# Scan stage: ScalarE's first tap issued in front of the older head's square, and the last output projection split, with its weights in another buffer

## The reference, cut to what matters

```python
H, P, N, G, K, CH, E = (32, 128, 128, 8, 4, 32, 256)   # 32 heads of width 128, 8 groups
proj = x @ in_proj_w.T                    # gate, (hidden, B, C), dt
hbc = silu(causal_conv(hbc, conv_w, K taps) + conv_b)
hs, B, C = split(hbc)
dt = softplus(dt + dt_bias)
# per head: a scan in chunks (inside a chunk by matmuls, from chunk to chunk by states)
y = (Y_diag + Y_off) + D * hs
h32 = y * silu(gate)                                  # per head, 1024 tokens x 128
g = h32.reshape(b, s, 8, 512)                         # 4 heads make one norm group
var = mean(g * g, axis=-1)
h32 = g * rsqrt(var + EPS)
return norm_w * h32 @ out_proj_w.T                    # 4096 -> 256, added to x
```

## Time and profile before

| | us |
|---|---|
| median of 3 runs | 1653.99 (1649.94 to 1654.58) |
| the profiled execution, its own time | 1655.48 |
| its span, first to last instruction | 1653.7 |
| share of the span in which PE, DVE, ACT, POOL were busy | 87%, 69%, 53%, 30% |
| the scan's heads in steady work (1010 to 1514 us): PE, DVE, ACT, POOL busy | 473.2, 387.6, 330.2, 290.3 of 504 |
| the end of the scan (1526 to 1549 us): PE, DVE busy | 17.4, 7.5 of 23 |

### The profile page before, as it was taken

One profiled execution on the slowest core, in us unless ns is written; L12 is line 12 of the kernel. 1 busy time (PEld: TensorE's weight loads), 2 busy tenths in 40 slices (PEclk: granted clock), 3 DMA queues, 4 the chain that ended last, 5 costly groups with the idle time before them and its releaser, 6 DMA issues. The chain is left out here.

```text
span 1653.7 us, 25033 instructions
## 1 busy us (share of the span) xinstructions
PE 1437.4 (87%) x7896; PEld 1056.5 (64%) x7896; DVE 1139.2 (69%) x2026; ACT 878.2 (53%) x1238; POOL 497.1 (30%) x407
## 2 busy tenths in 40 slices
PE   3999489999999966994997968899999999998697
PEld 3788343333333345883786757788887887887586
DVE  5622599989989847332775756777776777867475
ACT  2422227767767744322434765667575665755332
POOL 1444210000000113542001114655645556564100
PEclk9999759999999977997997998999999999999899
DMA  8532211111111028334001103222322222221200
GB/s 296 146 52 46 58 31 21 23 25 20 27 28 27 5 96 286 52 52 120 2 0 40 42 25 91 83 90 90 96 77 85 77 96 90 84 90 39 77 1 26
DMA packets 83030, 112.06 MB, mean 68 GB/s; under 512 B 11905, under 2 KB 60801, under 8 KB 82913
## 3 DMA queue, kind: packets, MB, share of 16 engines
q1 hardware_dynamic: 73152, 96.05, 19.5%
q0 software_dynamic: 9376, 14.16, 4.8%
q10 hardware_dynamic: 384, 0.39, 0.1%
HBM read 89.99 MB, written 11.93 MB: 62 GB/s over the span
## 5 line engine op out<-in xcount | busy, mean ns | idle before, releaser
L962 DVE TENSOR_REDUCE attn_max_chunks<-attn_scores 128x1 f32<-128x512 f32 x488 | 305.4, 684 | 30.7 <-PE attn_scores L1213 25.2
L1124 ACT ACTIVATE attn_probs<-attn_scoresT 128x1024 f32<-128x1024 f32 x256 | 248.2, 1022 | 118.8 <-PE attn_scoresT L1229 118.6
L1213 PE MATMUL attn_scores<-attn_k_picks,attn_q_group 64*128 64x512 f32 x488 | 188.5, 466 | 14.5 <-DVE attn_max_chunks L962 6.0
L1213 PEld LDWEIGHTS attn_scores<-attn_k_picks,attn_q_group 64*128 64x128 f32 x488 | 85.7, 191 | 178.5 <-DVE attn_max_chunks L962 170.4
L1644 DVE SCALAR_TENSOR_TENSOR ssm_scan_x<-ssm_scan_proj,ssm_w_conv,ssm_scan_x 128x1023 f32<-128x1023 f32 (+2 forms) x96 | 123.1, 1282 | 84.1 <-ACT ssm_scan_x L1639 78.4
L1229 PE MATMUL attn_scoresT<-attn_q_group,attn_k_picks 64*128 64x512 f32 x512 | 153.9, 438 | 3.3 <-ACT attn_probs L1124 3.3
L1241 PE MATMUL attn_o<-attn_probs,attn_v_group 128*32 128x512 f32 x1024 | 139.2, 616 | 0.4 <-ACT attn_probs L1124 0.3
L62 PE MATMUL ssm_scan_proj<-ssm_xnT_hi,ssm_w_in_hi 128*128 128x512 f32 x256 | 111.0, 434 | 27.8 <-DVE ssm_scan_x L1644 22.5
L293 POOL DMA_INDIRECT moe_sums<-moe_xn,moe_token x46 | 77.7, 1690 | 128.4 <-DVE moe_xn L430 122.6
L2481 PE MATMUL ssm_scan_out<-ssm_scan_w_out,ssm_scan_v 128*128 128x256 f32 x480 | 110.7, 384 | 4.6 <-POOL ssm_scan_w_out L2186 4.4
L481 ACT ACTIVATE moe_xnT<-moe_gate 128x512 f32<-128x512 f32 x46 | 27.5, 597 | 153.6 <-PE moe_gate L64 153.6
(11 more groups left out here) (355 smaller groups left out, 3400.5 us busy)
## 6 DMA issues: line engine op xcount, KB each, us to landing
ssm_cum_all<-ssm_cums SPq DMA_DIRECT2D x32, 512.0 KB, 3.7
ssm_scan_exp_cum<-ssm_cums SPq DMA_DIRECT2D x32, 512.0 KB, 3.7
moe_w_gate_lo<-in_moe_w SPq DMA_DIRECT2D x16, 512.0 KB, 11.2
moe_w_up_lo<-in_moe_w SPq DMA_DIRECT2D x16, 512.0 KB, 11.1
moe_w_down<-in_moe_w SPq DMA_DIRECT2D x16, 512.0 KB, 11.1
ssm_w_in<-in_in_w SPq DMA_DIRECT2D x64, 128.0 KB, 2.6
ssm_scan_w_out<-in_out_w SPq DMA_DIRECT2D x8, 512.0 KB, 3.8
moe_sums<-main_residual SPq DMA_DIRECT2D x2, 1024.0 KB, 5.6
```

Source lines behind the costliest of these rows:

```text
L962: return nc.vector.tensor_reduce(rmaxc[:, half, place:place + 1], chunk_bank(g, n), AX_X, ALU.max).then_inc(reduced, 1)
L1124: nc.scalar.activation(probs[s % 2][:, 2 * pair:2 * pair + 2, :], st_ps[pair][:], ACT.Exp, scale=SCALE).then_inc(exp_done, 1)
L1213: nc.tensor.matmul(chunk_bank(g, n), qs[b][head_rows(j), t * P:(t + 1) * P], kz[b][head_rows(j), j % 2, c * BANK:(c + 1) * BANK], start=Tr ...
```

## The change

First, in ACT's list `square` of head n-1 moves from behind `ahead(n)` to behind the first tap inside `ahead(n+1)`, so that tap comes in front of square. Second, the last group's output weights go to the buffer of `grow` (`w_out_last`), loaded once the last `cgrow` is done, and `scale_out(7)` scales them there. Third, PE's last projection first does heads 28 to 30 for pairs 0 and 1, then head 31 for them, then `norm_sums` into `y_ps`, then pairs 2 and 3.

```diff
+        w_out_last = grow[:].rearrange("p (j d) -> p j d", j=NORM_HEADS)
...
             def load_out(gw):
-                if after(gw, 1):
+                if is_at(gw, G - 1):
+                    sync.wait_ge(q["cgrow_done"], HM)
+                elif after(gw, 1):
                     sync.wait_ge(q["out_mm"], PAIRS * gw)
...
-                sync.dma_start(w_out[:], src).then_inc(w_out_in, 16)
+                sync.dma_start(w_out_last if is_at(gw, G - 1) else w_out[:], src).then_inc(w_out_in, 16)
...
-                nc.vector.tensor_copy(sums[:], out_ps[1][:, 0, 0:TT]).then_inc(q["sums_done"], 1)
+                nc.vector.tensor_copy(sums[:], y_ps[:, 0:TT] if is_at(gw, G - 1) else out_ps[1][:, 0, 0:TT]).then_inc(q["sums_done"], 1)
...
-            def ahead(n, j, gw, norm_of=None):
+            def ahead(n, j, gw, norm_of=None, square_of=None):
                 tap(n, j)
+                if square_of is not None:
+                    square(*square_of)
                 grow_of(n)
...
             def body(n, j, gw):
+                passed = (n - 1, (j - 1) % G, gw - (j % NORM_HEADS == 0)) if after(n, 1) else None
                 if not is_at(n, LAST):
-                    ahead(n + 1, j + 1, gw + (j % NORM_HEADS == NORM_HEADS - 1), gw - 1 if j % NORM_HEADS == 0 and after(n, 1) else None)
-                square(n, j, gw)
+                    ahead(n + 1, j + 1, gw + (j % NORM_HEADS == NORM_HEADS - 1),
+                          gw - 1 if j % NORM_HEADS == 0 and after(n, 1) else None, passed)
+                else:
+                    square(*passed)
...
             heads(act, body)
+            square(LAST, LAST % G, G - 1)
             norm(G - 1)
...
+            def project_last(p, heads_of):
+
+                first, end = heads_of[0] == 0, heads_of[-1] == NORM_HEADS - 1
+                for m in range(2):
+                    cols = slice((2 * p + m) * P, (2 * p + m + 1) * P)
+                    for jn in heads_of:
+                        last = nc.tensor.matmul(tail_ps[p][:, m, :], v[:, v_row((G - 1) % 2 * NORM_HEADS + jn), cols], w_out_last[:, jn, :],
+                                                start=(first and m == 0 and jn == 0), stop=(end and jn == NORM_HEADS - 1),
+                                                skip_group_check=True)
+                if end:
+                    last.then_inc(q["out_mm"], 1)
...
-            for p in range(PAIRS):
-                for m in range(2):
-                    project_out(G - 1, (G - 1) % 2, p, m, tail_ps[p])
-                if p == 0:
-                    norm_sums(G - 1)
+            pe.wait_ge(q["w_out_scaled"], G)
+            pe.wait_ge(q["v_done"], LAST)
+            pe.wait_ge(q["added"], PAIRS * (G - 1))
+            for p in range(2):
+                project_last(p, range(NORM_HEADS - 1))
+            pe.wait_ge(q["v_done"], HM)
+            for p in range(2):
+                project_last(p, (NORM_HEADS - 1,))
+            norm_sums(G - 1)
+            for p in range(2, PAIRS):
+                project_last(p, range(NORM_HEADS))
```

More of the change, by code:

```diff
@@ L2185, in scale_out @@
                 pool.wait_ge(w_out_in, 16 * (gw + 1))
-                nc.gpsimd.tensor_tensor(w_out[:], w_out[:], norm_w[:, bass.ds(gw * NORM_HEADS, NORM_HEADS)]
+                w = w_out_last if is_at(gw, G - 1) else w_out[:]
+                nc.gpsimd.tensor_tensor(w, w, norm_w[:, bass.ds(gw * NORM_HEADS, NORM_HEADS)]
                                         .unsqueeze(2).broadcast_to([P, NORM_HEADS, D]), ALU.mult).then_inc(q["w_out_scaled"], 1)
@@ L2460, in norm_sums, with project_out @@
                 pe.wait_ge(q["summed"], SUMS * (gw + 1))
-                if after(gw, 1):
+                if is_at(gw, G - 1):
+                    pe.wait_ge(q["y_done"], HM)
+                elif after(gw, 1):
                     pe.wait_ge(q["added"], PAIRS * gw)
+                dst = y_ps[:, 0:TT] if is_at(gw, G - 1) else out_ps[1][:, 0, 0:TT]
                 for t in range(TT):
-                    last = nc.tensor.matmul(out_ps[1][:, 0, t:t + 1], squares[:, t * P:(t + 1) * P], ones[:, 0:1],
+                    last = nc.tensor.matmul(dst[:, t:t + 1], squares[:, t * P:(t + 1) * P], ones[:, 0:1],
                                             start=True, stop=True)
                 last.then_inc(q["norm_mm"], 1)
-            def project_out(gw, b, p, m, out=None):
+            def project_last(p, heads_of):
[8 more added lines that the diff above has]
+                    last.then_inc(q["out_mm"], 1)
+            def project_out(gw, b, p, m):
                 if p == 0 and m == 0:
@@ L2471, in project_out @@
                     pe.wait_ge(q["v_done"], NORM_HEADS * (gw + 1))
-                if m == 0 and out is None and (p >= 2 or after(gw, 1)):
+                if m == 0 and (p >= 2 or after(gw, 1)):
                     pe.wait_ge(q["added"], PAIRS * gw + p - 1)
-                if m == 0 and out is not None and p == 0:
-                    pe.wait_ge(q["added"], PAIRS * gw)
                 if p == 1 and m == 0:
                     pe.wait_ge(q["sums_done"], gw + 1)
-                out = out_ps[p % 2] if out is None else out
+                out = out_ps[p % 2]
                 cols = slice((2 * p + m) * P, (2 * p + m + 1) * P)
```

## The result

Two comparisons on the chip, each with the kernel before beside it. In the first the changed kernel took 1630.32 us (median of 4, 1624.36 to 1631.37), before 1654.28, a ratio of 0.9835 [0.9803, 0.9867]. In the second it took 1627.88 us (median of 5, 1623.88 to 1631.66), a ratio of 0.9836 [0.9813, 0.9860]. By the ratios the change takes 27 us off (23 to 31 in the second comparison), by the medians 24.0 and, against 1654.34 for before, 26.5; 20.2 were forecast. The direction was right and the size too small. The profiled executions stand at 1653.7 and 1628.3 us of span, 25.4 apart.

A forecast was written before the change was run, and what follows sets the result against it. The prediction saw a circle through ACT, DVE and PE, with PE's floor at 15.14 us a head. Scan 13.7 plus end 6.5 made 20.2 us off: 1634 us, 8 in 10 within 1628 to 1643.

The forecast's parts named there:

- step 1: Heads 1 to 3: earlier taps cut PE's gaps from 3.40 to 2.43 us, gate projections stay slow; 2.9 us gained.
- the end: End of the scan: early last weights and new product order bring DVE's last additions 6.5 us earlier; bounds 4.5 and 6.8.
- heads 27 and 28: Written-out end of a group: the load starts from PE's quarter's end, so an earlier tap gains 0 us.
- Step 2: Loop middle heads: 16.07 us becomes 15.20, a gain of 0.87 in each of 8, 7.0 us.
- the circle: Chain through the heads: v, square and tap, DVE's taps, gate projection, chunk states, next v; forecast 0.97 us shorter.
- Step 3: Written-out middle heads: 15.33 to 15.20 us, 0.13 in each of 5, 0.65 us.
- Step 5: Last heads of groups: 2.4 us from three in the loop, 0.7 at its jump back, 0 from written-out ones.
- port term: Last loop heads: earlier `weigh` escapes POOL's scaling on DVE and POOL's shared SBUF ports; 0.83 us three times, about 2.4.
- jump back: Last head of a group at the loop's jump back: only loses PE's small waits, 0.7 us.
- the rivals: Four other outcomes: scan gain hidden 0.09, no gain at the end 0.07, full speed early 0.09, slower 0.04.
- the one on the full clock in the early heads: Heads 1 to 3: shorter gaps let gate projections run at full speed, 4.8 us more, 1629 us; chance 0.09.
- The slower case: Every head: earlier `weigh` starts behind a POOL product, each clash costing 1.69 us; 1663 us in all; chance 0.04.

The follow-up runs named there:

- e10_square_ahead: The changed kernel with the older head's square computed once more in front of the first tap; 1651.05 us, ratio to the kernel before 0.9955.
- e2_end: The kernel before with the change at the end alone (last weights in the growth buffer, new order of products); 1646.98 us, ratio 0.9947.
- first pair: The first profiles of the kernel before and of the changed kernel, compared; spans 1653.7 and 1628.3 us.
- e3_before: The kernel before run once more, unchanged; 1658.94 us, ratio 1.0014.
- e7_unrolled: The changed kernel with the loop over heads 8 to 23 written out; 1621.79 us, ratio to the kernel before 0.9778.
- e5_weigh_first: The kernel before with VectorE's two `weigh` multiplies moved forward by one addition, ScalarE untouched; 1651.28 us, ratio 0.9966.
- second pair: Profiles of a later, unchanged execution of the kernel before and of the changed kernel, compared; span 22.2 us shorter.

## Why the forecast was too small

The mechanism was right in its two halves, and e10_square_ahead and e2_end confirm them. What failed is the size of five terms, four of them too small. The largest shortfalls are step 1 and the end (1.2 and 1.3 us in the mean), where the sum missed what TensorE's clock costs behind a gap, and heads 27 and 28 (2.1 us), put at nothing.

- **Step 1, heads 1 to 3 (2.9).** The sentence "I keep the slow gate projection, since 2.43 is near 2.53" failed. Over all traces 20 of 21 projections behind the gap of 3.40 us were slow, and 6 of 18 behind the gap of 2.5, one of three in each trace. Three gaps shorter by 0.89 (2.7) and two projections faster by 1.6 (3.2), less 1.5 us that come back in head 3, most of it as the new wait of 1.23 for POOL, give the 4.3 of the first pair. Against e3_before, the one trace of before with a fast projection, it is 2.7; over all traces 4.1.
- **Step 2 (7.0) was too large by 1.0.** The step that failed is "the circle becomes 16.07 - 0.97 = 15.10". The tap starts 0.23 us behind v where square started 0.03 behind it, and DVE's idle time before its taps fell by 0.74 us (2.35 to 1.61), not by 0.97. 16.07 - 0.74 is 15.33, the measured length: the circle is the bound still, not PE's floor, which was read rightly (15.14 against the 15.11 of e7_unrolled, where the loop is written out and the tap starts 0.1 us behind v). Why the tap starts later in the loop is not shown. Heads 13 and 21, at 16.43 before, gained 0.75 as well.
- **Step 3 (0.65).** Six heads, not five, went from 15.33 to 15.11, not 15.20: 1.3 us.
- **Step 5.** The port term came out at 2.4 us, as forecast, but that is partly luck: heads 11 and 19 gained 0.6 each and head 23 1.2, where 0.83 each was reckoned, and they stopped at 17.0 and not at 16.76. e5_weigh_first shows its cause apart. The rule of the Trainium skill ("SBUF — State Buffer", section "SBUF: two separate sides"), that one engine holds the shared ports for its whole instruction, fits 1.28 against 2.98 us, and it also names what is left: POOL's one-column addition of 0.2 us takes 1.17 while DVE's `v` runs, and `v` takes 2.51 behind POOL's product. What failed is "an earlier tap doesn't shorten the written-out ones". Head 7 gained 0.15. Head 27 with head 28 took 36.1 to 36.9 us in five looped traces with the late tap and 34.5 in the sixth, e10_square_ahead, against 33.6 to 34.2 in the three with the early tap and POOL's scaling: 2.1 us less in the mean. In the earlier trace rows the 2.53 us of waiting for `xend` and the slow work behind it were both there to be read. But written out the two heads took 34.7 with the late tap and 35.7 with the early one. So how much of the 2.1 is the tap's and how much the clock's luck stays open. Most of the 5.0 us at the jump back in the first pair belong to no step; in the second pair it is the forecast 0.7, and the means of all traces with the stall lie 1.4 apart.
- **The end (6.5).** The profile that I reckoned from had the mild form of the old end (27.27 us), and against it 6.45 was right. Two of five traces have 30.5 and 30.6, since PE has a low granted clock for both pairs behind the gap (0.54 and 0.66 in e3_before). The mean is 7.8 us, and the interval of e2_end, 5 to 13, holds it.

The terms as the traces give them on average are 4.1, 6.0, 1.3, 2.4, 1.4, 2.3 (heads 7, 27 and 28) and 7.8, in all 25.3 us, inside the 23 to 31 that the second comparison allows. So about 5 us were missing in the forecast, half of them (1.2 in step 1, 1.3 at the end) in what PE does behind a gap. Between this sum and the measured 27 stay 2 us, less than either interval.

Of the rivals none came true as a whole; the one on the full clock in the early heads did so in two heads of three. The slower case is refuted: `weigh` met no product of POOL, though `v` did.

## What to carry to other kernels

- A gap of TensorE costs its length and what the clock takes behind it. Where a wait of 2.5 to 4.5 us goes away or gets a quarter shorter, reckon that part as well, from several stretches of the profile rather than from one.
- One profile is one draw: compare stretches between two executions of the same kernel before a difference is put down to the change. Here a stall of 3.8 us was there or not, the old end took 27.3 or 30.6 us, and heads 27 and 28 differed by 2.4 us between kernels with the same order there.
- ScalarE, or whatever releases the longest chain, should do first what the chain waits for; work that only a far consumer needs comes behind. The next bound then is the engine with the longest list in the odd heads, here POOL with the scaling of the weights.

## What the runs showed that I had not expected

- At the loop's jump back TensorE stands still for 3.4 to 4.7 us (eight of ten traces, none of the three without a loop), always with nine more packets of the instruction queue than in the two without it, and in the loop DVE's three dependent taps take 4.13 instead of 3.92 us. Written out, before gained 17 us by it (0.9896), nearly as much as the swap.
- Behind the three early gaps of 2.5 us the clock is low in one place in each of six traces, and not in the same place. What decides it is not shown.
- Products of 0.22 us take 0.42 each for up to 6.7 us behind a gap of 4.4 us, and a later gap of 0.26 us in the same stretch was followed by slow ones again (5.41 us for 16).
